# First routing tile of a gated cross-attention and expert block: three orders of work written out by hand are changed

## What is computed

```python
kv = (ctx @ W_kv.T + b_kv).reshape(B, S, 16, 16, 2); k, v = kv[..., 0], kv[..., 1]
qh = layernorm(x).reshape(B, S, 16, 16)
attn = softmax(einsum('bshd,bstd->bsht', qh, k) / 4)        # heads against heads, within a token
context = einsum('bsht,bstd->bshd', attn, v).reshape(B, S, 256)
x = x + tanh(g_xattn) * (context @ W_out.T + b_out)
xn = layernorm(x)
probs = softmax(einsum('ntd,ed->nte', xn, gate_w))           # 8 experts
g, m = top_k(probs.transpose(0, 2, 1), 64)                   # per sequence and expert: 64 of 256 tokens
h = gelu(xn[batch_idx, m] @ w1) @ w2                         # 256 -> 1024 -> 256 for each expert
x = x + tanh(g_ffn) * zeros.at[batch_idx, m].add(g[..., None] * h)
```

## Time and profile before

| | us |
|---|---|
| median of 3 runs | 693.37 |
| lowest, highest | 689.89, 695.35 |
| the profiled execution, its time | 693.32 |
| the profiled execution, its span | 691.2 |
| TensorE busy in it | 655.4 |
| VectorE busy in it | 593.9 |
| GpSimd busy in it | 532.3 |
| ScalarE busy in it | 456.1 |

### The profile page before, as it was taken

How to read it: one execution, slowest core, us unless ns; L and a number is a source line. 1 busy time by engine, 2 the same in 40 slices (tenths; PEclk the granted TensorE clock), 3 DMA queues, 4 the chain that set the end, 5 groups by cost and what they waited for, 6 DMA issues and landing times.

```text
span 691.2 us, 11552 instructions
## 1 busy us (share of the span) xinstructions
PE 655.4 (95%) x3873; PEld 537.3 (78%) x3873; DVE 593.9 (86%) x775; ACT 456.1 (66%) x1140; POOL 532.3 (77%) x498
## 2 busy tenths in 40 slices
PE   7989999989799999989999999989999999999995
PEld 4556566656688888878888888868888899999995
DVE  6999999997999999989999999899999357565762
ACT  6677777773777777867777778757666545444542
POOL 4899999997868888988888889888888626545233
PEclk9899999999999999999999999999999999999998
DMA  4976698552668888776788877767887878999972
GB/s 133 307 252 215 227 300 271 199 198 78 213 194 264 233 267 237 220 220 181 233 242 249 245 242 221 215 198 236 232 234 227 273 197 270 281 291 313 313 182 30
DMA packets 95455, 157.79 MB, mean 228 GB/s; under 512 B 8091, under 2 KB 73382, under 8 KB 95398
## 3 DMA queue, kind: packets, MB, share of 16 engines
q1 hardware_dynamic: 82390, 139.63, 60.7%
q0 software_dynamic: 12288, 16.79, 13.1%
q10 hardware_dynamic: 720, 0.66, 0.3%
HBM read 123.48 MB, written 33.55 MB: 227 GB/s over the span
## 4 chain that ended last, share of the span: by engine, by line
PE 60%; DMA 12%; DVE 11%; issue 9%; POOL 4%; ACT 2%; SPq 0%; POOLq 0%; ACTq 0%; DVEq 0%
PE bank L1313 21%; PE bank L1331 19%; DMA out_dram<-ys,ids 7%; DVE prod_v L533 4%; PE bank L1234 4%; DVE co L537 3%; PE bank L1254 3%; PE bank L1187 2%; PE bank L1293 2%; DMA w1in<-w_parts 2%; DVE prod_s L551 2%; PE bank L1342 2%; DMA xg<-xn_scratch,ids 1%; PE bank L1266 1%; POOL prod_p L381 1%
## 5 line engine op out<-in xcount | busy, mean ns | idle before, releaser
L1313 PE MATMUL bank<-xin,w1in 128*128 128x256 f32 x1392 | 185.9, 291 | 5.5 <-issue 3.0
L1313 PEld LDWEIGHTS bank<-xin,w1in 128*128 128x128 f32 x1392 | 175.4, 196 | 7.3 <-issue 6.0
L1331 PE MATMUL bank<-w2s,hT 128*128 128x256 f32 x704 | 161.1, 382 | 0.0
L457 POOL DMA_INDIRECT out_dram<-ys,ids x64 | 102.4, 1600 | 73.2 <-DVE ys L734 49.9
L1331 PEld LDWEIGHTS bank<-w2s,hT 128*128 128x128 f32 x704 | 130.5, 190 | 16.1
L537 DVE TENSOR_REDUCE co<-prod_v 128x208 f32<-128x3328 f32 (+2 forms) x32 | 109.4, 3420 | 1.1
L533 DVE TENSOR_TENSOR prod_v<-bank,Ex 128x3328 f32<-128x3328 f32 (+2 forms) x32 | 109.3, 3414 | 0.1
L954 ACT ACTIVATE hT<-bank 128x512 f32<-128x512 f32 x128 | 76.0, 596 | 47.3 <-PE bank L1313 47.0
L440 POOL DMA_INDIRECT xg<-xn_scratch,ids x64 | 66.8, 1043 | 33.4 <-issue 17.0
L389 POOL TENSOR_TENSOR tree_a<-prod_p 128x512 f32<-128x512 f32 (+3 forms) x64 | 85.0, 1329 | 4.7
L381 POOL TENSOR_TENSOR prod_p<-kvs,q 128x1024 f32<-128x1024 f32 (+3 forms) x28 | 77.9, 2781 | 9.1 <-ACT q L904 7.5
(11 more groups left out here) (176 smaller groups left out, 1214.9 us busy)
## 6 DMA issues: line engine op xcount, KB each, us to landing
w1in<-w_parts SPq DMA_DIRECT2D x112, 512.0 KB, 4.6
w2s<-in_L_ffn_w_dram SPq DMA_DIRECT2D x27, 1024.0 KB, 5.7
w_parts<-w1s SPq DMA_DIRECT2D x32, 512.0 KB, 3.3
w1raw<-in_L_ffn_w_dram SPq DMA_DIRECT2D x32, 256.0 KB, 4.4
w_more<-w_parts SPq DMA_DIRECT2D x12, 512.0 KB, 5.8
out_dram<-x SPq DMA_DIRECT2D x32, 128.0 KB, 4.2
xn_scratch<-xn SPq DMA_DIRECT2D x32, 128.0 KB, 2.6
w1raw<-in_L_ffn_w_dram SPq DMA_DIRECT2D x4, 1024.0 KB, 7.2
```

The source lines that it names most:

```text
L457: pool.indirect_dma_start(out=out_rows[:, :], out_offset=bass.IndirectOffsetOnAxis(ap=ids[:, g % 2, p * E + e:p * E + e + 1], axis=0), in_ ...
L1313: ins = pe.matmul(HB[k % 2][:, D * f:D * (f + 1)], w1q[:, w, c, P * f:P * (f + 1)].bitcast(f32r), xin[:, n % 2, x_, c, :], start=(m == 0), ...
L1331: ins = pe.matmul(YB[:, D * p:D * (p + 1)], hT[:, n % 2, f, cols], w2s[:, n % 2, f, :], start=(f == 0), stop=(f == FC - 1))
```

## The change

On TensorE, within step 10, the logits of tile 8 and route_columns(0) go ahead of ahead_kv(2), the third projection for a later tile, and score_sums(11) goes ahead of ahead_kv(3). On ScalarE, take_logits(8) goes ahead of the exponentials, take_kva(2) behind take_gates(0), and x2_stats(9) ahead of take_kva(3). On GpSimd, gather(1) moves from behind values(10) to behind scores(11) and rsqrt(13), so that in step 11 it stands directly ahead of gather(2). Nothing is added or left out.

```diff
--- before.py
+++ after.py
@@ -496,12 +496,14 @@
                 scores(s)
                 if not routing(s):
                     rsqrt(s + 2)
+                if s == N0:
+                    gather(1)
                 rows_out(s)
                 first_rows_in(s)
                 if not routing(s):
                     rows_in(s)
                 values(s)
-                if routing(s):
+                if routing(s) and s >= N0:
                     rows_in(s)
             rsqrt(NT + 2)
             gather(n1 + 1)
@@ -1064,13 +1066,13 @@
             take_caT(2)
             take_kva(1)
             take_caT(3)
-            take_kva(2)
+            take_logits(s - 2)
             exponentials(s)
             take_gates(0)
+            take_kva(2)
             take_kv(s + 1)
-            take_logits(s - 2)
+            x2_stats(s - 1)
             take_kva(3)
-            x2_stats(s - 1)
             take_xh(0)
             s = N0
             take_ctT(s + 1)
@@ -1435,11 +1437,11 @@
             ahead_transposes(2)
             ahead_kv(1)
             ahead_transposes(3)
+            logits(s - 2)
+            route_columns(0)
             ahead_kv(2)
-            route_columns(0)
-            logits(s - 2)
+            score_sums(s + 1)
             ahead_kv(3)
-            score_sums(s + 1)
             token_transposes(0)
             s = N0
             ctx_transposes(s + 1)
```

## The result

| | before | changed |
|---|---|---|
| median of 15 executions, us | 693.48 | 688.69 |
| lowest, highest | 689.89, 696.73 | 685.5, 695.1 |
| span of the profiled execution | 691.2 | 686.5 |

The ratio is 0.9946, 95% interval 0.9925 to 0.9966: 3.7 us less, between 2.4 and 5.2. The forecast was 689.2, 4.1 us less. In the terms of the chances it is "within 1%".

What follows compares the result with a forecast made beforehand. The prediction took one idle place on TensorE in step 11 as what the change could shorten: 2.64 us from an earlier reduction plus 1.47 us of clock, 4.1 us, so 693.3 - 4.1 = 689.2 us, range 685.7 to 695.0.

Steps and rivals of the forecast that it cites:

- within 1%: Whole kernel: a time change of less than 1% (6.9 us) either way, chance 0.91.
- The bound: Step 11: TensorE idles 2.42 us before hidden(0, 2), through a chain of ScalarE, VectorE and GpSimd.
- The ids: Step 10, VectorE: ids start at 158.2 instead of 159.65, a gain of 1.45 us.
- score_sums' margin of 0.17 us: Step 10, TensorE: products ready at 159.84, score_sums(11) needs them by 160.01; booked 0, at most 0.3 us.
- TensorE's order at no cost: Step 10: the sum of TensorE's work is unchanged, token_transposes(0) stays at 165.89; cost 0.
- ScalarE's order at no cost: Step 10: moved copies have readers after 165.89, take_kva(3) ends at about 166.6; cost 0, otherwise 0.6 us.
- gather(1) in 2.8 us: Step 11: second issue at 171.35, 1.8 us ahead of the w1 load, landed at 174.15; margin 0.6 us.
- The clock, 1.47 us: Step 11, hidden(0, 2) and (0, 3): with about 0.4 us idle the clock is not cut, 1.47 us gained.
- The rival that it would be cut anyway: Step 11: the clock is cut all the same, only 2.64 us gained, 690.7 us; chance 0.20.
- Sum: TensorE at the end of hidden(0, 3): 2.64 + 1.47 = 4.1 us earlier, expected to last to the end.
- The gather behind the load: Step 11: gather(1) meets the w1 load, lands after 5.3 us; 692.6 to 691.1 us, middle 691.9; chance 0.15.
- the prediction's price was 1.6: Step 11, slower rival: gather(1) lands after 7.6 us, low clock stays, 693.3 + 1.6 = 694.9 us; chance 0.08.

Runs made afterwards that it cites:

- experiment 1: TensorE's and ScalarE's new order alone, against the changed kernel with gather(1) put back where it was; 690.63 us, ratio 0.9966.
- experiment 2: Against the kernel before, only gather(1) moved behind the scores, TensorE's and ScalarE's order as before; 692.96 us, ratio 0.9999.
- experiment 7: Against the changed kernel, route_columns moved ahead of hidden(n, 2) in steps 18 and 26; 686.38 us, ratio 0.9901.
- changed again: The changed kernel profiled a second time, with no edit; 688.43 us, ratio 0.9931.
- Experiment 4: The kernel before, TensorE's idle time ahead of hidden(0, 2) filled with 18 transposes whose result nobody reads; 691.05 us, ratio 0.9974.

## Why the prediction was right, point by point

- *The bound.* Right: one idle place in step 11, and a chain through ScalarE, VectorE and GpSimd. Experiments 1 and 2 move the parts of that chain separately by 1.5 and 2.0 us at the reduction, 1.45 and 2.1 expected.
- *The ids.* 158.12 for 158.2, and VectorE's subtraction is what ends last, not route_columns.
- *score_sums' margin of 0.17 us.* It held in this trace: 160.24 on TensorE with no wait in front of it, the products being done at 158.52 + 1.23 = 159.75. It does not always hold. In the traces of the new order in which VectorE's lists came later (last section), score_sums starts 0.05 to 0.25 us later from the mark (3.55 to 3.75 for 3.50), in experiment 7 behind a wait of 0.18 us for VectorE's products. That is the 0.15 us between changed and changed again.
- *TensorE's order at no cost.* Here a term was too small. The prediction gave ahead_kv(2) the 2.04 us that it had in front of route_columns; in front of score_sums it takes 2.23 (158.01 to 160.24), as a projection did there before (160.01 to 162.22, 2.21). ahead_kv(3) takes 2.13, so token_transposes(0) starts at 166.04 instead of 165.89, and its four transposes take 0.66 us for 0.60.
- *ScalarE's order at no cost.* take_xh(0) starts at 166.74 instead of 166.53. That is 0.04 us behind the end of the transposes, the same as before (165.89 + 0.60, then 166.53). take_kva(3) ends at the same moment, 166.75; that it adds anything is not shown. The low part starts at 167.37, not at 167.15, and these 0.2 us went into the reduction (170.57 for 170.27) and hidden(0, 2) (175.71 for 175.40).
- *gather(1) in 2.8 us.* Right, 2.7 to 2.8, and right that the w1 load decides it: the three other distances from the load gave 3.7, 4.3 and 5.2 us. One reading was wrong: the load at 173.16 lies ahead of both issues of gather(2) (173.89 and 175.23), not between them and the landing. The Trainium skill's DMA: Bandwidth & Descriptors (Queues, rings and completion order) lets one expect a gather slowed beside a load but not queued behind all of it. The landings alone, which the prediction took as agreeing, do not tell: in experiment 2 the rows were there 3.75 us behind the load's issue, and such a load itself lands in 3.2 us in the trace of before. The packets of that trace do not agree for the first load. q0 carries the indirect DMAs, q1 SyncE's loads; the first line is 173.5 to 176.5 us, where q0 is absent, the other two are 176.5 to 180:

```profile
q1 hardware_dynamic: 158, 0.58, 68.7%
q1 hardware_dynamic: 418, 0.73, 55.1%
q0 software_dynamic: 95, 0.26, 32.1%
```

  gather(1)'s second issue at 166.49 had its first packets at 168.0, 1.5 us later. gather(2)'s first issue at 173.89 has none before 176.5, 2.6 us later, and by then q1 has moved 0.58 MB, more than one whole load. Behind that the two queues move side by side. Why the rows' packets waited is not shown.
- *The clock, 1.47 us.* Experiment 4 measured 1.48 with everything else in place. The rival that it would be cut anyway did not come about; 1.12 us of idle (experiment 1, one trace) did not bring it either.
- *Sum.* 4.1 expected at step 12, 3.8 and 3.6 measured; the difference is TensorE's 0.2 us above, with what it made of the reduction. It lasts: VectorE's ids of step 18 come 3.7 us earlier (296.41 for the 300.11 of the earlier trace rows), hidden(8, 0) 3.3. The 0.4 us between these are no loss of the change, since the second traces of both kernels swap it (125.11 and 125.53 us from step 12 to hidden(8, 0) before, 125.65 and 125.19 changed). The median's 4.8 is above the sum and its ratio's 3.7 just below; the cuts of the later steps, which I used only for the range, are of the size of that difference.
- *The rivals.* The gather behind the load is a real mechanism, missed by the order of two issues: with the half change it took what was gained, and with gather(1) last it made step 12 1.3 us later than before, on which the prediction's price was 1.6. The sum's 2.8 us had no better ground than the 1.8 us that the prediction counted between issue and load (2.3 measured). No row then said how near is too near; at 1.0 us it was 3.2 and 3.7 us. That the distance was enough was in part luck.

## What to carry to other kernels

When an indirect gather is put behind other work, look not only at when its reader comes but at the next large load that another queue will issue: here a gather landed in 2.8 us when issued 2.3 us ahead of it and in 5.2 when issued 0.7 behind it. In its new place alone it gave 2.0 us at the reduction, of which 1.0 reached step 12 and nothing showed in the time. When TensorE stands idle in a stretch of light work, price the matmuls behind the gap at their lower clock too; it was 1.5 of 3.8 us here. And where a producer's result goes to another engine on the longest chain, try it in front of long independent work (experiment 7), and count the short wait that this makes.

## What the hardware showed that was not expected

- The clock cuts behind the waits of 2 to 3 us in pieces at the steps 19 and 27 come in half of the cases (9 of 18 groups, 4.4 to 4.6 us instead of 3.1), with the same program there and nearly the same gaps. The one in 141 to 146 us came in 7 of the 12 traces. Behind the single gap of 2.42 us in step 11 it came in both traces of the kernel before.
- VectorE's cast of the 64x64 indices to fp32 in the first routing step took 0.65 to 0.67 us in five traces and 1.24 to 1.45 in seven. These seven are just the ones with TensorE's low clock in 141 to 146 us (granted 0.66 to 0.72 there, 1.00 in the five). How a stretch of TensorE's clock some 10 us earlier and the length of a VectorE instruction hang together is not shown. In changed and in changed again:

```profile
154.45 0.65 DVE L672 CAST top_f<-top_i 64x64 f32<-64x64 uint32 x1
155.67 1.33 DVE L672 CAST top_f<-top_i 64x64 f32<-64x64 uint32 x1
```

  It moved VectorE against TensorE by 0.6 us there. In the kernel before step 12's position did not follow (before filled, with the long one, has hidden(0, 2) at 21.27 like before, with the short one), since VectorE waited for route_columns in any case. In the changed kernel only the half microsecond between the products and score_sums covers it, and 0.15 us came through.
